# A two-layer block on one core: own feed-forward buffers, the norm guard on GpSimd, band products of two sequences in one, and a new step order

## The reference, cut to what matters

```python
# x: 16 sequences of 256 tokens of 128 values; c: 16 x 128
mod = (silu(c) @ wmod).reshape(16, 6, 1, 128)          # sa, ca, ga, sb, cb, gb
h = layernorm(x) * (1 + ca) + sa
x = x + ga * guided(h, guidance)                       # 64 guides; steps h[t+1]-h[t]; a band of 8 steps back
h = layernorm(x) * (1 + cb) + sb
for l in range(2):                                     # ffn_ref
    g = shift_token(h)                                 # second half of the channels, one token back
    q, k, v = split(g @ wqkv[l], 3)                    # 8 heads of 64
    q, k = rotary(l2norm(q) * qs, l2norm(k) * ks)      # l2norm divides by max(norm, 1e-12)
    h = h + local_attention(q, k, v) @ wo[l]           # windows of 64, and the window before
    g = layernorm(shift_token(h)) * lg + lb
    a, b = split(g @ w1[l] + b1[l], 2)                 # 341 values each
    h = h + (a * gelu(b)) @ w2[l] + b2[l]
out = x + gb * h
```

## Time and profile before

| | us |
|---|---|
| median of 3 runs | 883.07 (880.1, 888.11, 883.07) |
| the profiled execution | 880.0 |
| its span, first to last instruction | 878.2 |
| TensorE busy | 759.0 |
| VectorE busy | 695.8 |
| ScalarE busy | 657.4 |
| GpSimd busy | 552.3 |

### The profile page before, as it was taken

The page is one execution under the profiler, slowest core; times in us unless marked ns, Lnnn a source line. Parts: engine busy times, 40 slices in busy tenths (PEclk is TensorE's granted clock), DMA queues, the critical chain, the costliest instruction groups (busy, mean ns, idle before and its releaser), DMA issues.

```text
span 878.2 us, 20446 instructions
## 1 busy us (share of the span) xinstructions
PE 759.0 (86%) x7439; PEld 561.1 (64%) x7439; DVE 695.8 (79%) x1639; ACT 657.4 (75%) x1545; POOL 552.3 (63%) x358
## 2 busy tenths in 40 slices
PE   2888879897999998889989989889889999888884
PEld 2676657665676765666767766666667666566653
DVE  3669977787998987688989987687989975877842
ACT  2254857888897977878878877877796887688773
POOL 1257754596876771586985781496897671867801
PEclk9799999999999999999989999999999999999996
DMA  7000000000000000000000000000000000000000
GB/s 232 1 13 5 9 2 2 1 2 1 2 2 1 26 1 26 1 2 1 1 2 1 25 1 25 2 2 1 1 1 1 14 1 14 1 2 2 2 13 13
DMA packets 12716, 10.08 MB, mean 11 GB/s; under 512 B 1089, under 2 KB 11721, under 8 KB 12617
## 3 DMA queue, kind: packets, MB, share of 16 engines
q1 hardware_dynamic: 12616, 8.77, 3.2%
HBM read 6.67 MB, written 2.10 MB: 10 GB/s over the span
## 4 chain that ended last, share of the span: by engine, by line
PE 36%; DVE 26%; ACT 14%; issue 13%; POOL 9%; DMA 2%; SPq 0%; POOLq 0%; DVEq 0%; ACTq 0%
PE pair L858 5%; PE dense L1017 5%; ACT probs L1167 4%; DVE space L1611 4%; PE mixed L904 4%; DVE q_norm L1616 3%; POOL roots L1688 3%; DVE qk L1413 3%; PE dense L979 3%; PE pair L944 3%; PE dense L980 2%; PE dense L981 2%; DVE neg_max L1431 2%; POOL qk L1740 2%; DVE space L1609 2%
## 5 line engine op out<-in xcount | busy, mean ns | idle before, releaser
L1740 POOL TENSOR_TENSOR qk<-space 128x512 f32<-128x512 f32 x128 | 173.7, 1370 | 35.7 <-DVE q_norm L1616 34.5
L1688 POOL TENSOR_TENSOR roots<-powers,minus_half 128x16 f32<-128x16 f32 (+1 forms) x65 | 189.1, 2918 | 7.2 <-DVE powers L1625 5.9
L1167 ACT ACTIVATE probs<-pair,neg_max 128x128 f32<-128x128 f32 x512 | 139.9, 403 | 6.0 <-DVE neg_max L1431 5.0
L1732 POOL TENSOR_TENSOR space<-space,tables 128x512 f32<-128x512 f32 x64 | 88.0, 1378 | 38.1 <-ACT space L1295 38.0
L1099 PE MATMUL dense<-wq_hi,h_hi 128*128 128x512 f32 x192 | 91.2, 475 | 23.9 <-DVE space L1611 15.7
L1611 DVE TENSOR_TENSOR space<-dense,tables 128x512 f32<-128x512 f32 x128 | 87.2, 681 | 20.3 <-ACT space L1295 20.3
L1413 DVE TENSOR_TENSOR qk<-qk,roots 128x1024 f32<-128x1024 f32 x64 | 93.8, 1480 | 5.1 <-POOL roots L1688 5.1
L1291 ACT ACTIVATE squares<-dense 128x512 f32<-128x512 f32 x128 | 77.8, 609 | 23.0 <-PE dense L1101 15.8
L1431 DVE TENSOR_REDUCE neg_max<-pair 128x4 f32<-128x512 f32 x128 | 81.8, 683 | 15.7 <-PE pair L944 15.5
L858 PE MATMUL pair<-eye_s,probs 128*128 128x128 f32 x512 | 75.7, 284 | 13.0 <-ACT probs L1167 12.7
L1616 DVE TENSOR_REDUCE q_norm<-squares 128x8 f32<-128x512 f32 x128 | 86.3, 674 | 0.0
(11 more groups left out here) (210 smaller groups left out, 1837.3 us busy)
## 6 DMA issues: line engine op xcount, KB each, us to landing
x_in<-n_L_attn_embeddings_dram SPq DMA_DIRECT2D x8, 256.0 KB, 2.8
out_dram<-hn SPq DMA_DIRECT2D x8, 256.0 KB, 2.2
qk<-in_L_ffn_wqkv_dram SPq DMA_DIRECT2D x1, 1536.0 KB, 8.3
qk<-in_L_ffn_w_dram SPq DMA_DIRECT2D x1, 682.0 KB, 10.5
wo_s<-in_L_ffn_wo_dram SPq DMA_DIRECT2D x2, 256.0 KB
o_t<-in_L_wmod_dram SPq DMA_DIRECT2D x1, 384.0 KB, 4.2
band_s<-const_band_dram SPq DMA_DIRECT2D x1, 256.0 KB, 4.4
probs<-const_rotary_dram SPq DMA_DIRECT2D x1, 256.0 KB, 8.9
```

The costliest lines, as they stand in the source:

```text
L1167: last = act.activation(probs[:, ring, hh, :], banks[m][:, hh * P:(hh + 1) * P], ACT.Exp, bias=neg_max[:, ring, hh:hh + 1], scale=1.0)
L1688: return pool.tensor_tensor(to, of, minus_half[0:of.shape[0], 0:of.shape[-1]], ALU.pow)
L1732: pool.tensor_tensor(raw, raw, rot(layer, t, 2 * m), ALU.mult).then_inc(cosine_part, 1)
L1740: pool.tensor_tensor(qk[s][:, t, m * INNER:(m + 1) * INNER], turned_c[:, t % 2, m, :], turned_s[:, t % 2, m, :], ALU.add).then_inc(added, 1)
```

## The change

- `hn_hi`, `hn_lo` and `hidden` are tiles of the feed-forward alone; `space`, `turned_c` and the GELU ring are gone. The cosine part is written straight into `qk`, GELU straight into `hidden`, and the sums and products are formed in place.
- `proj.tile` and `ff.up` wait for the rounded half, and for the low half only before the third product, which for `ff.up` is now the product with the low half.
- The maximum with 1e-24 goes from VectorE's list (64 steps) to GpSimd's `unit_root`; VectorE's sum of squares is written straight into `powers`.
- GpSimd's sum into `qk` waits until the bank is emptied, and no longer for the sum of squares.
- In `new.sum` the banks hold one tile position k for both sequences, not one sequence; the band products cover both sequences at once.
- `step_t` lies in the space of `weighed`, its last column is cleared for each unit, and the squares' unused output goes into `h_a`.
- `ORDER` and `BANK_OF_USE` are written anew. The steps are the same but for VectorE's 64 `proj.rsqrt`.

```diff
+        hn_hi, hn_lo = sb("hn_hi", [P, UNIT], F32R), sb("hn_lo", [P, UNIT], F32R)
-        space = sb("space", [P, 8 * UNIT])
...
+        turned_s = sb("turned_s", [P, 2, 2, UNIT])
+        hidden = sb("hidden", [P, 3, UNIT])
...
-        def wait_halves_free(eng, i, slot, kind):
...
+        def ff_before(i, slot):
+
+            return (i, slot - 1) if slot else (i - 1, 3)
...
-                    pe.wait_ge(ff_lo, before + 1)
+                    pe.wait_ge(ff_hi, before + 1)
...
+                    pe.matmul(to, w1_hi[:, layer, cols], hn_hi[:, :], start=True, stop=False)
+                    pe.matmul(to, w1_lo[:, layer, cols], hn_hi[:, :], start=False, stop=False)
+                    pe.wait_ge(ff_lo, before + 1)
+                    done(pe.matmul(to, w1_hi[:, layer, cols], hn_lo[:, :], start=False, stop=True), i, slot, step)
...
+                    for k in range(2):
...
+                        both = to[:, 0:2 * VS].rearrange("p (m n) -> p m n", m=2)[:, :, 0:P + 1]
+                        pe.matmul(both, band_s[:, 0, k * P:(k + 1) * P], z.weighed[:, 0::2, 0:P + 1], start=True,
+                                  stop=False, skip_group_check=True)
+                        if k:
+                            pe.matmul(both, band_s[:, 1, P:SEQ], z.weighed[:, 1::2, 0:P + 1], start=False,
                                       stop=False, skip_group_check=True)
+                        for m in range(2):
                             j = 2 * m + k
+                            last = pe.matmul(to[:, m * VS:m * VS + P], z.guide_mix[:, j * P:(j + 1) * P], guides[:, :],
                                              start=False, stop=True, skip_group_check=True)
...
-                pe.wait_ge(qkv_lo, before + 1)
+                pe.wait_ge(qkv_hi, before + 1)
...
+                pe.wait_ge(qkv_lo, before + 1)
                 done(pe.matmul(to[:, :], h_lo[:, rows], wq_hi[:, layer, cols], start=False, stop=True), i, slot, step)
...
-                    if slot > 1 and runs(i, slot, (PROJ, "split"), turns):
-
-                        act.wait_ge(added, 8 * (proj(i, slot)[1] + 1))
-                    if chunk == 2:
-                        act.wait_ge(*read_at(i, slot, (FF, "up", 0, 1)))
+                    if chunk == 0 and before > 0:
+                        act.wait_ge(*filled_at(*ff_before(i, slot), (FF, "down", 0)))
...
-                            if past(2 * tau + m - 3):
-                                act.wait_ge(added, 2 * tau + m - 3)
-                            last = act.activation(turned_c[:, t % 2, m, :], src[:, :], ACT.Copy)
+                            if past(tau - 7):
+                                act.wait_ge(turned[m], tau - 7)
+                            last = act.activation(qk[s][:, t, m * INNER:(m + 1) * INNER], src[:, :], ACT.Copy)
...
-                    dve.tensor_reduce(q_norm[:, 16 * (t % 2) + 8 * m:16 * (t % 2) + 8 * m + 8],
+                    if past(tau - 3):
+                        dve.wait_ge(qk_rooted, tau - 3)
+                    dve.tensor_reduce(powers[:, t, 8 * m:8 * m + 8],
...
-                    dve.tensor_scalar(powers[:, t, :], q_norm[:, 16 * (t % 2):16 * (t % 2) + 16], 1e-24, None,
-                                      ALU.max).then_inc(qk_powered, 1)
...
+                sums = powers[:, tau % 4, :]
+                pool.wait_ge(summed, 2 * tau + 2)
+                pool.tensor_scalar(sums, sums, 1e-24, None, ALU.max).then_inc(qk_powered, 1)
                 pool.wait_ge(qk_powered, tau + 1)
...
+                    pool.memset(z.step_t[:, :, SEQ - 1:SEQ], 0.0)
...
-                        pool.wait_ge(summed, 2 * tau + m + 1)
-                        pool.tensor_tensor(qk[s][:, t, m * INNER:(m + 1) * INNER], turned_c[:, t % 2, m, :],
-                                           turned_s[:, t % 2, m, :], ALU.add).then_inc(added, 1)
+                        pool.wait_ge(*read_at(i, slot, (PROJ, "tile", t, m)))
+                        part = qk[s][:, t, m * INNER:(m + 1) * INNER]
+                        pool.tensor_tensor(part, part, turned_s[:, t % 2, m, :], ALU.add).then_inc(added, 1)
```

The lists change in this manner (TensorE, turn 1, slot 0, the beginning):

```diff
-        1/0:a.turn.1.1 1/0:a.turn.0.0 0/3:a.project 1/0:a.turn.1.0 1/0:a.score.0 1/0:a.score.1 1/0:ff.stats
-        1/0:a.flip.0.0 0/3:proj.tile.3.2 1/0:a.flip.0.1 1/0:a.mix.0.0 1/0:a.flip.1.0 1/0:a.flip.1.1 1/0:ff.norm
...
+        1/0:a.turn.0.0 1/0:a.turn.1.0 0/3:a.project 1/0:a.score.0 1/0:a.score.1 1/0:ff.stats 0/3:proj.tile.3.2
+        1/0:a.flip.0.0 1/0:a.flip.0.1 1/0:a.flip.1.0 1/0:a.flip.1.1 1/0:a.mix.0.0 1/0:a.mix.0.1 1/0:ff.norm
```

More of the change, by code:

```diff
@@ L58 @@
[L58 to L62, removed]
@@ L68 @@
[L68 to L72, removed]
@@ L73 @@
[L73 to L102, removed]
@@ L345 @@
-        1/2:new.again 1/2:ff.up.1 1/2:new.stream 1/2:ff.up.0 1/3:a.score.0.0 1/3:a.score.0.1 1/3:a.score.1.0
-        1/3:a.score.1.1 1/2:ff.up.2 1/2:proj.unit.2 1/2:proj.unit.3 1/2:ff.down 1/3:proj.split 1/2:a.project
-        1/2:store.turn 1/2:proj.keep 1/3:proj.tile.0.0 1/3:a.mix.0.0 1/3:new.stats 1/3:proj.tile.0.1
-        1/3:proj.tile.1.0 1/3:a.mix.0.1 1/3:a.mix.1.0 1/3:a.mix.1.1 1/3:proj.rsqrt.0 1/3:proj.tile.1.1 1/3:new.turn
-        1/3:proj.tile.2.0 1/3:proj.tile.2.1 1/3:a.score.2.0 1/3:proj.rsqrt.1 1/3:proj.rsqrt.2 1/3:a.score.2.1
@@ L370 @@
-        2/2:a.score.3.1 2/2:proj.tile.2.1 2/2:ff.stats 2/2:proj.unit.0 2/2:a.mix.2.0 2/2:a.mix.2.1 2/2:ff.norm
-        2/2:proj.rsqrt.2 2/2:proj.tile.3.0 2/2:proj.tile.3.1 2/2:proj.rsqrt.3 2/2:proj.unit.1 2/2:ff.hi
-        2/2:a.mix.3.0 2/2:a.mix.3.1 2/2:new.gate 2/2:new.again 2/2:ff.up.0 2/2:new.stream 2/2:ff.up.2 2/2:ff.up.1
-        2/2:proj.unit.2 2/3:proj.split 2/2:ff.down 2/3:a.score.0.0 2/3:a.score.0.1 2/3:a.score.1.0 2/3:a.score.1.1
-        2/2:store.turn 2/3:proj.tile.0.0 2/2:proj.keep 2/3:proj.tile.0.1 2/3:proj.rsqrt.0 2/2:proj.unit.3
@@ new lines @@
+        1/3:a.mix.3.0 1/3:a.mix.3.1 1/3:new.dots 1/3:new.sims 1/3:ff.norm 1/3:new.weights 1/3:ff.hi 1/3:proj.unit.1
+        1/3:a.project 1/3:proj.tile.3.1 1/3:new.gate 1/3:ff.up.0 1/3:ff.up.1 2/0:a.score.0.0 2/0:a.score.0.1
+        1/3:ff.up.2 1/3:new.again 1/3:ff.down 2/0:a.score.1.0 2/0:a.score.1.1 1/3:store.turn 2/0:ff.stats
+        1/3:new.stream 2/0:ff.norm 2/0:a.mix.0.0 2/0:a.mix.0.1 1/3:proj.keep 2/0:ff.hi 2/0:a.mix.1.0 2/0:a.mix.1.1
+        1/3:proj.unit.2 2/0:ff.up.0 2/0:ff.up.1 2/0:ff.up.2 1/3:proj.unit.3 2/0:ff.down 2/0:proj.split
@@ new lines @@
+        2/3:proj.tile.3.0 2/3:proj.tile.3.1 2/3:proj.unit.1 2/3:ff.hi 2/3:a.mix.3.0 2/3:a.mix.3.1 2/3:new.gate
+        2/3:new.again 2/3:ff.up.1 2/3:ff.up.2 2/3:proj.unit.2 2/3:ff.up.0 2/3:new.stream 2/3:a.project 2/3:ff.down
+        3/0:a.score.0.0 3/0:a.score.0.1 3/0:a.score.1.0 3/0:a.score.1.1 2/3:store.turn 3/0:ff.stats 3/0:ff.norm
+        3/0:a.mix.0.0 2/3:proj.keep 3/0:a.mix.0.1 3/0:ff.hi 3/0:a.mix.1.0 3/0:a.mix.1.1 2/3:proj.unit.3 3/0:ff.up.0
+        3/0:ff.up.2 3/0:ff.up.1 3/0:ff.down 3/0:a.score.2.0 3/0:proj.split 3/0:a.score.2.1 3/0:a.score.3.0
```

864 lines of the change are left out of this document (430 added, 434 removed).

## The result

The changed kernel takes 829.02 us (median of four runs, 828.6 to 831.28) against 881.59 for the kernel before on the same chips: ratio 0.9405, 95% interval 0.9339 to 0.9471. The profiled execution has a span of 826.8 us.

A forecast was written before the change was run, and what follows sets the result against it. The prediction saw no full engine but four lists worked off in order, the late engine changing from step to step. Its terms summed to -17.2 us, giving 862.8 us profiled and 866 for the median, range 845 to 886.

The forecast's parts named there:

- All steps in a new order, -4: All engines' lists and banks: a better fit recovers some idle TensorE time, -4 us, bounds -15 and +15.
- Guards, -5.5 and +2.5: 64 maxima moved from VectorE to GpSimd: -5.5 us on the chain for VectorE, +2.5 for clamps before GpSimd's roots.
- The low half, -5: Projections and feed-forward: TensorE runs two products before waiting for the low half, -5 us, bounds 0 and -18.
- The sum without the reduction, -1: GpSimd's sum into qk no longer waits for VectorE's row reduction: -1 us, bounds 0 and -23.
- GELU, -1: Feed-forward: GELU of chunk 2 no longer waits for VectorE's product of chunk 0, -1 us, bounds 0 and -13.9.
- Band products, -3: Sum stage: six band products become three of 258 columns, 0.83 us less per unit, -3 us, bounds 0 and -8.5.
- (a): Rival: time only changes hands, TensorE being late next; 875 us profiled, 878 for the median; chance 0.26.
- (b): Rival: VectorE co-limits throughout, so all its guards and the waits on it go; 835 us; chance 0.10.
- (c): Rival: GpSimd becomes the bound, all 64 clamps on the path at 0.64 us, +41; 904 us; chance 0.12.
- (d): Rival: the order of steps alone outweighs all edits, bound 15 us either way; no chance of its own.
- the signs of being right: VectorE some 20 us less busy, clamp 0.2 to 0.4, third product awaiting h_lo, TensorE's idle some 15 us smaller, among others.
- the signs of being wrong: A clamp above 0.5 us, GpSimd full in more stretches than one, or TensorE's wait for emptied banks above 15 us.

The follow-up runs named there:

- sums_behind_dots: The changed kernel with GpSimd's roots right behind new.dots moved behind the next two sums in five units: 838.99 us, ratio 0.9539.
- edits_old_order: All edits of the change, run with the lists and banks of the kernel before (less VectorE's 64 guard steps): 866.32 us, ratio 0.9848.
- start_old: The changed code with old lists and banks up to the first a.project and new ones behind it: 841.41 us, ratio 0.958.
- The two cuts at the first and the one at the sixth: Changed code, lists and banks switching at the first a.project (new then old 855.81 us, old then new 841.41) or the sixth (new then old 847.53).
- no_guard: The changed kernel without GpSimd's clamp and its wait for itself, the maximum with 1e-24 left out: 833.32 us, ratio 0.947.
- guard_back_late: The changed kernel with the guard back on VectorE, three steps later than right behind its tile's second row sum: 853.37 us, ratio 0.9695.
- band_back: The changed kernel with band products one sequence at a time again, six instead of three per unit: 829.94 us, ratio 0.9439.
- mix_pool: All edits with only GpSimd's list new, the other three lists and the banks old: 863.49 us, ratio 0.984.

## Why the prediction was wrong

**All steps in a new order, -4, is the step that failed.** The runs gave -37. Two of its arguments fell. The first took the steps' small displacement, 1.3 places on average, as a sign of a small effect: counted in places, an exchange of a root and two sums is nothing, and sums_behind_dots lost 10 us by such exchanges in five units. The second took the largest group of waits as a bound, as though a list could only mend one group. It mends many. Waits of TensorE in edits_old_order, from 75 to 840 us and over the run, and VectorE's unit_length by form there:

```profile
PE dense L1075 <- DVE turned_s L1588: 12.5, 18, 3.3
```
```profile
PE pair L838 <- DVE qk L1387: 11.5, 14, 1.8
```
```profile
L1387 DVE TENSOR_TENSOR qk<-qk,roots 128x1024 f32<-128x1024 f32 x64 | 95.2, 1499 | 9.4 <-POOL roots L1654 9.4
```

After, the first is 6.9, the second is down to 2.2, and unit_length waits 1.0 us for roots instead of 9.4 and takes 1287 ns instead of 1499: 12.9 us less of the same 64 instructions. In all VectorE is 33.3 us less busy than in edits_old_order with as many instructions. That it was held by GpSimd's work I had read only for the guard. The start was not looked at either: the argument drew on the idle time between 75 and 850 us. In the kernel before, TensorE stands there for 10.0 us at a stretch (us, times, longest):

```profile
PE dense L1041 <- POOL step_t L1719: 10.0, 1, 10.0
```

ScalarE's old list has the rounding of the projections' weights (`setup.hi`), which waits for a DMA, ahead of the first unit's `new.turn`, from which GpSimd forms the steps; the new list has it behind `new.dots`. ScalarE in edits_old_order and in the changed kernel:

```profile
15.36 2.85 ACT L1112 ACTIVATE wq_hi<-qk 128x1536 fp32r<-128x1536 f32 x2 [12.64 <-DMA qk<-in_L_ffn_w_dram]
18.12 1.00 ACT L1212 ACTIVATE h_a<-dense,mod 128x256 f32<-128x256 f32 x2
```
```profile
10.25 1.02 ACT L1216 ACTIVATE h_a<-dense,mod 128x256 f32<-128x256 f32 x2 [7.52 <-PE dense L842]
```

The first unit's `new.turn` starts 7.9 us earlier, and TensorE's long wait is gone; this exchange was not run by itself. The beginning of edits_old_order and of start_old, by stretch, against the first row of the changed kernel's stretches above:

```profile
0.00:75.00 75.00, 49.97 (x277) 40.42 (x278) 45.04 (x133) 25.32 (x64) 32.93 (x42) 0.91 0.24 72
```
```profile
0.00:75.00 75.00, 47.93 (x286) 39.17 (x286) 46.44 (x136) 25.36 (x64) 34.45 (x44) 0.98 0.24 72
```

By 75 us TensorE has 383 records instead of 277, of which 140 in either kernel are warm-up transposes. The first record of each a.project on TensorE tells where the gain is made:

| start us of a.project | 1st | 4th | 6th | 16th |
|---|---|---|---|---|
| edits_old_order | 130.3 | 279.5 | 370.9 | 839.4 |
| after | 117.6 | 259.9 | 350.6 | 798.1 |
| ahead | 12.7 | 19.6 | 20.3 | 41.3 |

A third is made before the first, another 7 us up to the fourth, and the rest at up to 4 us in each later slot. The two cuts at the first and the one at the sixth agree with it (10.5 to 12.4, 18.8). The granted clock in the first 75 us is 0.98 against 0.91, but in these executions that is little of the 12.7: start_old, with the old beginning, was granted 0.98 as well, has 286 records by 75 us, and starts its first a.project at 128.3, 2.0 us before edits_old_order.

**The edits** were forecast at -13.2 together (the sum without the order) and gave -14.5 in the old lists. That the two sums are so near is in part luck: the guards by themselves gave 7.3 for a forecast of 3.0, which leaves some 7 for the rest, forecast at 10.2, if the parts add. Term by term:

- Guards, -5.5 and +2.5. In the old lists they gave -7.3. The clamp was sized rightly (0.293 for 0.29), but of its +2.5 on the chain nothing shows (no_guard). The rule of the Trainium skill that was weighed there (GPSIMD Engine Reference, section 4.1 Engine selection) gives such work to VectorE. On the price of one clamp the trace agrees that GpSimd is the slower, a median of 252 ns on GpSimd against VectorE's undisturbed 174; for the run it does not, since the move made both orders faster. In the new lists the guard's move is worth 24.7, above the bound of 23.3: there the guards on VectorE would take 35.1 us beside sums that start earlier, or make the roots wait (guard_back_late).
- The low half, -5: worth 9.4 in the new lists, inside the bound of 18. 2.5 us of waits on h_lo (L1082) are left.
- The sum without the reduction, -1: a gain of 6.8 with the guard on GpSimd, and a loss of 11.7 with it on VectorE. The prediction priced the two edits as separate; they are not.
- GELU, -1: of the 16.0 us for which ScalarE is idle ahead of GELU 15.5 now end with TensorE's product and none with VectorE's, which had 13.9; but the edit could not be undone alone.

```profile
L1196 ACT ACTIVATE hidden<-dense,columns 128x512 f32<-128x512 f32 (+1 forms) x48 | 32.7, 689 | 16.0 <-PE dense L988 15.5
```

- Band products, -3. A stage took 3.70 us at 323 us and takes 2.79 at 112, so 0.91 for the 0.83 forecast; the reason was wrong, since joining saves nothing that shows (band_back 0.9, within the noise) and by the pieces above the outer loop does it. The memset took 0.10, as counted.

**The rivals.** (a), that TensorE is the next one late, is refuted: its idle time from 150 us to the last 30 or so fell from 69.3 to 44.5 us, and its share of the chain hardly moved (36% to 37%). (b) came nearest in its time, 835, and in part by its mechanism, VectorE held throughout, though most of what it summed lay elsewhere. (c) needed 0.31 us per clamp on the path; the clamps take 0.293, and by no_guard they cost the run nothing. (d), that the order outweighs the edits, is what happened, 37 to 14.5, and its bound of 15 was taken from one row.

**The signs.** Of the signs of being right all came, VectorE's and TensorE's larger than forecast (53.0 us less busy for 20; 24.8 us less idle for 15). Of the signs of being wrong one came: in steps of 25 us GpSimd is busy for more than 24 us in five stretches, where before it was so in one, and the kernel was faster all the same. The sign that was named for the order, a wait for emptied banks above 15 us, did not come (6.9), though the order set most of the time.

What stays open: which exchanges of the new lists make the rest of the 37 beyond the start and the roots behind the dots, and how they divide between waits that end sooner and operations that are no longer held. In mix_pool 21 us less on VectorE gave 2.8 at most, so time given back on one engine is worth little by itself; that it pays where the other three lists can use it is a reading, not shown.

## What to carry to other kernels

Where the engines work off fixed lists, price a new order by all waits and all held operations together, the start included, not by the largest wait or by the number of places moved; a run of the changed code under the old lists and a cut in time tell it apart cheaply. Price two edits that touch the same pair of engines together: an operation that starts earlier on GpSimd can make VectorE's neighbour longer, and taking that neighbour away is then worth more than its undisturbed time (here 24.7 us for 64 guards of 0.17).
